# The halo copy moved behind the pair operation in both recurrences of an alignment, with two further semaphores in the backward one

## The reference

```python
x = x + tanh(g_xattn[0]) * L0_xattn(ctx_1024, layernorm(x))   # time warping alignment
x = x + tanh(g_ffn[0])   * L0_ffn(layernorm(x))               # 64 experts, top 8
x = x + tanh(g_xattn[1]) * L1_xattn(layernorm(x), ctx, ctx)   # 16 heads over 77 keys
x = x + tanh(g_ffn[1])   * L1_ffn(layernorm(x))               # 8 experts, top 2
```

```python
R[i, j] = D[i, j] + min(R[i-1, j], R[i, j-1], R[i-1, j-1])     # row_step, col_step
choice  = argmin([R[i-1, j-1], R[i-1, j], R[i, j-1]])          # backtrack, one cell at a time
expanded[j] += small[i]                                        # for every cell (i, j) of the path
```

## Time and profile before

| what | value |
|---|---|
| median of 3 runs | 836.29 us (835.22 to 840.12) |
| profiled execution, its time | 840.12 us |
| profiled execution, its span | 838.4 us |
| busy in the span: PE, DVE, ACT, POOL | 681.6, 629.8, 409.6, 414.6 us |
| share of the chain that ended last: PE, DVE | 70%, 19% |

### The profile page before, as it was taken

The page is one execution under the profiler, slowest core; times in us unless marked ns, Lnnn a source line. Parts: engine busy times, 40 slices in busy tenths (PEclk is TensorE's granted clock), DMA queues, the critical chain, the costliest instruction groups (busy, mean ns, idle before and its releaser), DMA issues.

```text
span 838.4 us, 13196 instructions
## 1 busy us (share of the span) xinstructions
PE 681.6 (81%) x3114; PEld 544.3 (65%) x3114; DVE 629.8 (75%) x2092; ACT 409.6 (49%) x751; POOL 414.6 (49%) x450
## 2 busy tenths in 40 slices
PE   4423210089999999999999879999998999999996
PEld 2211110077788888888888559998866888888884
DVE  6779999778777777777777786767585777777774
ACT  2534300034565656565656554445454565656563
POOL 5657730026566666666666451110134666666663
PEclk9755555557999999999999979999599999999999
DMA  5365421124877777777777100000417676657661
GB/s 131 72 138 143 124 68 32 34 52 94 162 153 144 158 140 156 141 149 148 153 144 156 34 10 1 1 0 0 94 33 158 138 159 142 156 140 158 143 145 51
DMA packets 79209, 89.14 MB, mean 106 GB/s; under 512 B 44181, under 2 KB 56838, under 8 KB 75716
## 3 DMA queue, kind: packets, MB, share of 16 engines
q1 hardware_dynamic: 72118, 78.37, 44.8%
q0 software_dynamic: 4320, 9.68, 4.1%
q10 hardware_dynamic: 2734, 0.69, 0.4%
HBM read 79.84 MB, written 8.70 MB: 106 GB/s over the span
## 4 chain that ended last, share of the span: by engine, by line
PE 70%; DVE 19%; issue 5%; DMA 2%; ACT 2%; POOL 1%; DVEq 0%; POOLq 0%; ACTq 0%
PE bank L1000 14%; PE bank L1002 13%; PE bank L1001 13%; PE bank L1136 7%; PE bank L1134 6%; PE bank L1133 6%; PE bank L1064 4%; DVE arena L1432 3%; PE bank L1046 2%; DVE arena L1428 2%; DVE arena L1389 2%; DVE arena L1381 1%; DVE arena L1429 1%; PE bank L939 1%; DVE arena L1390 1%
## 5 line engine op out<-in xcount | busy, mean ns | idle before, releaser
L694 POOL TENSOR_TENSOR act_lo<-arena,act_hi 128x512 fp32r<-128x512 f32 x232 | 300.2, 1294 | 201.9 <-ACT act_hi L831 201.9
L1644 DVE TENSOR_TENSOR bank<-arena,bank 128x512 f32<-128x512 f32 x232 | 160.7, 693 | 105.2 <-PE bank L1002 72.3
L843 ACT ACTIVATE arena<-bank 128x512 f32<-128x512 f32 x232 | 138.9, 599 | 178.1 <-PE bank L1002 176.0
L1000 PE MATMUL bank<-xn_hi,w_hi 128*128 128x512 f32 x464 | 187.3, 404 | 3.6 <-DVE arena L1652 3.6
L1002 PE MATMUL bank<-xn_lo,w_hi 128*128 128x512 f32 x464 | 184.8, 398 | 0.0
L1001 PE MATMUL bank<-xn_hi,w_lo 128*128 128x512 f32 x464 | 184.2, 397 | 0.0
L1652 DVE TENSOR_TENSOR arena<-bank,arena 128x512 f32<-128x512 f32 x232 | 160.4, 691 | 21.5 <-DVE bank L1644 9.2
L831 ACT ACTIVATE act_hi<-arena 128x512 fp32r<-128x512 f32 x232 | 145.2, 626 | 15.7 <-DVE arena L1652 15.7
L1000 PEld LDWEIGHTS bank<-xn_hi,w_hi 128*128 128x128 f32 x464 | 88.4, 191 | 27.4 <-DVE arena L1652 5.4
L1002 PEld LDWEIGHTS bank<-xn_lo,w_hi 128*128 128x128 f32 x464 | 88.3, 190 | 22.0
L1001 PEld LDWEIGHTS bank<-xn_hi,w_lo 128*128 128x128 f32 x464 | 88.7, 191 | 20.8
(11 more groups left out here) (194 smaller groups left out, 963.8 us busy)
## 6 DMA issues: line engine op xcount, KB each, us to landing
arena<-scr_mask SPq DMA_DIRECT2D x94, 512.0 KB, 6.4
scr_w<-prep_out POOLq DMA_DIRECT2D x25, 192.0 KB, 2.2
w_raw<-scr_w SPq DMA_DIRECT2D x25, 192.0 KB, 6.5
arena<-scr_one SPq DMA_DIRECT2D x6, 512.0 KB, 6.0
w_raw<-in_L_ffn_expert_gate_k SPq DMA_DIRECT2D x32, 64.0 KB, 6.1
w_raw<-in_L_ffn_expert_up_k SPq DMA_DIRECT2D x32, 64.0 KB, 5.9
w_raw<-in_L_ffn_expert_down_k SPq DMA_DIRECT2D x64, 32.0 KB, 5.4
prep_in<-in_L_ffn_wg POOLq DMA_DIRECT2D x21, 64.0 KB, 2.3
```

Source lines behind the costliest of these rows:

```text
L694: nc.gpsimd.tensor_tensor(act_lo[:, k % 2, :], act_a[:, k % 2, :], act_hi[:, k % 2, :].bitcast(F32), ALU.subtract).then_inc(FF[f]["alo"], 1)
L843: nc.scalar.activation(act_s[:, k % 2, :], ps[4 + k % 2][:], ACT.Silu).then_inc(FF[f]["silu"], 1)
L1000: nc.tensor.matmul(out, w_h, x_h, start=start, stop=False)
L1644: nc.vector.tensor_tensor(ps[6 + i][:], act_s[:, i, :], ps[6 + i][:], ALU.mult).then_inc(FF[f]["t"], 1)
```

## The change

In the forward loop the pair minimum goes first and the halo copy second; the scan now waits for the halo copy (`s_halo`) instead of the pair minimum. In the backward loop the pair sum goes first and the halo copy second, with a semaphore of its own (`s_bhalo`); the pair sum waits for the last scan and for the last halo copy, and the scan waits for three things: the thresholds (`s_thr`), the pair sum (`s_pair`) and the halo copy (`s_bhalo`).

```diff
-                nc.vector.stream_shuffle(cur[:, 0:1], prev[:, CW:CW + 1], shift)
-                nc.vector.tensor_tensor(mst[:, s % MST, :], prev[:, 1:CW + 1], prev[:, 0:CW], ALU.min).then_inc(s_upper, 1)
+                nc.vector.tensor_tensor(mst[:, s % MST, :], prev[:, 1:CW + 1], prev[:, 0:CW], ALU.min)
+                nc.vector.stream_shuffle(cur[:, 0:1], prev[:, CW:CW + 1], shift).then_inc(s_halo, 1)
                 nc.vector.tensor_tensor(lg[:, s, 1, :], prev[:, 0:CW], prev[:, 1:CW + 1], ALU.is_le)
-                dve.wait_ge(s_upper, s + 1)
+                dve.wait_ge(s_halo, s + 1)
                 nc.vector.tensor_tensor_scan(cur[:, 1:CW + 1], mst[:, s % MST, :], dl[:, s, :], cur[:, 0:1],
                                              ALU.min, ALU.add).then_inc(s_scan, 1)
...
                 nc.vector.scalar_tensor_tensor(thr[:, s0:s1, :], lg[:, s0:s1, 0, :], 2.0, lg[:, s0 + 1:s1 + 1, 1, :],
-                                               ALU.mult, ALU.max)
+                                               ALU.mult, ALU.max).then_inc(s_thr, 1)
...
                 if k >= 1:
                     dve.wait_ge(s_exit, k)
-                nc.vector.stream_shuffle(qex[:, slot, CW:CW + 1], qex[:, slot + 1, 0:1], back)
+                    dve.wait_ge(s_bhalo, k)
                 nc.vector.tensor_tensor(pair[:, slot, :], qex[:, slot + 1, 0:CW], qex[:, slot + 1, 1:CW + 1],
                                         ALU.add).then_inc(s_pair, 1)
+                nc.vector.stream_shuffle(qex[:, slot, CW:CW + 1], qex[:, slot + 1, 0:1], back).then_inc(s_bhalo, 1)
+                dve.wait_ge(s_thr, 1 + max(0, k - AHEAD + PIECE) // PIECE)
                 dve.wait_ge(s_pair, k + 1)
+                dve.wait_ge(s_bhalo, k + 1)
                 nc.vector.tensor_tensor_scan(qex[:, slot, 0:CW][:, ::-1], pair[:, slot, :][:, ::-1], thr[:, slot, :][:, ::-1],
                                              qex[:, slot, CW:CW + 1], ALU.add, ALU.is_gt).then_inc(s_exit, 1)
```

More of the change, by code:

```diff
@@ L339, in program @@
         s_dld = [sem(f"dist_lanes{b}") for b in range(B)]
-        s_upper = sem("wave_upper")
+        s_halo = sem("wave_halo")
         s_scan = sem("wave_row")
         s_steps = sem("wave_steps")
+        s_thr = sem("back_thresholds")
         s_pair = sem("back_pairs")
+        s_bhalo = sem("back_halo")
         s_exit = sem("back_exits")
```

## The result

The changed kernel takes 847.46 us (median of 4 runs, 845.70 to 850.66) against 835.75 for the kernel before (834.41 to 840.12): ratio 1.0136, 95% interval 1.0093 to 1.0178. It is 11.7 us slower; 841.8 was forecast, and the range ended at 847.0.

What follows compares the result with a forecast made beforehand. VectorE alone was taken to bound both loops, with PE behind them. Forward 0 and backward +5.5 us on the median 836.29 gave 841.8 us, +0.66%, with a range of 836.5 to 847.0.

Steps and rivals of the forecast that it cites:

- Where the time is decided: Both loops: VectorE alone sets their length, so a microsecond there moves the start of what follows by a microsecond.
- The forward part: Forward loop: swapping pair minimum and halo copy costs 0.00 a step, with an end of 0.01, 0.9 us.
- the next instruction can start 0.10 behind it: Forward step: the halo copy was taken to start 0.10 us behind the pair minimum's start.
- The backward part, the kind of cost: Backward scan: its wait instruction can be passed only when the halo copy has ended, which delays the scan.
- The backward part, its size: Backward loop: pair sum to scan 0.34 in place of 0.28, 0.06 a step, 5.5 us.
- 0.09 for end to start over the wait instruction: Backward step: 0.09 us from the halo copy's end to the scan's start, read from a later stage's wait.
- The prediction's own sign of being wrong: Ahead of the backward scan: a gap of 0.04 or over 0.12, or copy and mask load standing apart.
- The rest of that term: Backward step, pair sum to scan: 0.10 to the halo copy's start and 0.152 for the copy, besides the wait.
- The wait ahead of the pair sum at nothing: Backward loop: the wait for the last halo copy costs nothing; without cover, up to 9.1 us.
- The mask load: Both loops: LOAD_MASK_SELECT between pair operation and halo copy taken at nothing; at 0.03 a step, 2.8 us in each loop.
- The rivals of the other sign: Waits are free, 836.3 to 837.2 us, chance 0.12; or each step's scan-to-scan chain shortens by 0.06, 825.3 us, chance 0.03.
- The second rival: Mask load costs 0.03 in 184 steps, or backward wait instruction over 0.09; 847.3 or 851 us, chance 0.15.

Runs made afterwards that it cites:

- Run 3: Changed kernel with the backward scan's three waits written halo copy first, so the scan carries the halo wait; 1.9 us over the kernel before, ratio 1.0022.
- run 5: Changed kernel with the backward halo copy ahead of the pair sum again, all added waits kept; 6.8 us over the kernel before, ratio 1.0082.
- run 8: Kernel before with a long-met thresholds wait carried by the backward scan, the pair sum's moved to a wait instruction; 6.0 us over the kernel before.
- run 4: Changed kernel with the wait instruction ahead of the backward scan looking at the pair sum first, halo copy second; 5.7 us over the kernel before.
- run 6: Changed kernel without the wait for the last halo copy ahead of the backward pair sum; 10.0 us over the kernel before, ratio 1.0113.
- run 7: Changed kernel with only the halo wait, on the backward scan, and no halo wait ahead of the pair sum; 1.9 us over the kernel before.
- run 10: Kernel before with three long-met waits added ahead of the backward scan, so two wait instructions stand there; 10.3 us over the kernel before.

## Why the prediction was wrong

- **Where the time is decided:** right. VectorE sets the length of both loops (the 42.55 us for which GpSimd is busy beside the forward one don't), and what is lost there (11.3 us by the scans) starts the rest later one for one (store of the path 11.45 later). The medians differ by 11.7, so that what is behind gave back nothing that they can tell.
- **The forward part:** taken at 0.00, with an end of 0.01 a step; measured 0.009, 0.9 us, the upper end. What was off is "the next instruction can start 0.10 behind it": it is 0.12 (50.69 to 50.81), with the mask load between. The pair minimum itself starts 0.32 behind the scan and not 0.33, which gives a part back.
- **The backward part, the kind of cost:** right. The loss is the wait instruction that can be passed only behind the newest result. Run 3 shows it with the order and all waits held, run 5 with the order turned back, and run 8 with a single added wait in the kernel before.
- **The backward part, its size:** this is the step that failed, and with it the 841.8. "0.09 for end to start over the wait instruction" was read from the earlier trace rows, "the same form of wait". The form was the same, the order in it not: there the newest semaphore stands second, here first. Measured 0.13, and run 4, which only turns the two, brings back the 0.09 and takes 0.042 a step off, 3.8 us by the traces (6.0 by the medians, each against the kernel before on its chip). The backward loop lost 10.4 us where 5.5 were forecast; 0.04 x 92 = 3.7 us of the missing 4.9 are in this term. The prediction's own sign of being wrong, a gap over 0.12 in front of the backward scan, is what came. The order was to be seen in the built program before any run, and I didn't ask whether it mattered.
- **The rest of that term:** 0.12 for 0.10 ahead of the copy, less the 0.01 of the pair sum's earlier start, is some 0.01 a step, 0.9 us. The five long steps make 0.75 us more. The parts are rounded and add up to a little over 4.9. Why those five are long, no run settles; with one wait instruction less a step, run 6 has two, 0.04 and 0.07 over their kind, and with neither of them run 7 has none.
- **The wait ahead of the pair sum at nothing:** right for the regular steps; by run 6 it makes 0.6 us through the long ones.
- **The mask load:** the 0.03 of the earlier trace rows in each of 184 steps didn't come. Load and copy start together in the steps shown; what came is 0.02 ahead of both.
- **The rivals of the other sign:** the waits weren't free, since the one ahead of the scan is for the newest count, and the ring wasn't shortened, since the halo copy ends 0.27 behind the pair sum's start (111.90 to 112.17) and is what the scan hangs on.
- **The second rival,** "the wait instruction costs more than 0.09 from end to start", is what happened, with a chance of 0.15, and its price was set at the wrong part: it named 0.19 from the earlier trace rows, a form with a register operation. Its other price, 847.3 with the mask load's 0.03 in each step, lies next to the measured 847.46 by luck, since the mask load made none of it. The range ended at 847.0, 0.5 under the median.
- **The page of the Trainium skill,** "VectorE: DVE Perf Modes", section "The DRAIN you can't avoid", says of chained copies that the semaphore after each costs nothing extra: this case agrees for a wait that is long met (run 6), and disagrees for the newest one on a wait instruction of its own (run 8, 6.0 us for 92 of them). No run here takes the scan's wait away altogether.

## What to carry to other kernels

In a chain of short instructions that each need the last one's result, ask for each wait not only whether it is met but where it sits: the wait that is met last belongs on the instruction itself, the long-met ones on the wait instruction ahead, and if two share that one, the later met second. In this kernel the order of three lines of code decided between 1.9 us and 11.7 us, with the same waits and the same instructions. An added wait that is never waited for can cost by moving another one off its seat; compare the built program's waits, not the code's.

## What of the hardware was not expected

A wait instruction on VectorE with one semaphore took 21 ns in every case here; none with two took under 49. With two it depends on which is met last: 50 where the newest stands first (the changed kernel, run 10), 83 in the median in run 4, 104 in run 5 and 223 in run 3, where it begins at its first semaphore and stands under the work. Where it was the last thing ahead of the scan, the scan started 0.045 us behind its end in the median. So a newest result cost, from its end to the scan's start, 0.036 with the wait on the scan, 0.090 as the second of two on a wait instruction, 0.104 alone on one, and 0.133 as the first of two. Behind a pair operation that starts when a wait is passed, LOAD_MASK_SELECT and STREAM_SHUFFLE start 0.12 us later, where another operation of 32 columns followed after 0.10.
